# Last stage of a four-stage kernel: a new common order of steps, conditional waits between scatter-adds, tile loads ahead of the last store

## What is computed

```python
xf = x.reshape(-1, D)                                  # 4096 tokens, D = 256, after a layernorm
scores = jax.nn.softmax((xf @ gate_w.T).astype(jnp.float32), axis=-1)
top_vals, top_idx = jax.lax.top_k(scores, K)           # K = 2 of E = 8
w_dense = jnp.zeros((T, E), x.dtype).at[jnp.arange(T)[:, None], top_idx].set(weights)
h = jnp.einsum('td,ehd->teh', xf, W1)
y, g = jnp.split(h, 2, axis=-1)
eo = jnp.einsum('teh,edh->ted', y * jax.nn.silu(g), W2)
z = jnp.einsum('te,ted->td', w_dense, eo)
z = z + _gated_mlp(xf, Ws1, Ws2)
x = x + jnp.tanh(g_ffn[1]) * z
```

## Time and profile before

| quantity | value |
|---|---|
| median of 3 runs | 1089.26 us (1087.65 to 1091.56) |
| profiled execution | 1092.42 us |
| its span, from first to last instruction | 1090.7 us |
| busy in the span: PE, DVE, ACT, POOL | 958.1, 765.4, 574.4, 400.7 us |
| mean granted clock of PE | 0.937 of full speed |

### The profile page before, as it was taken

One profiled execution on the slowest core, in us unless ns is written; L12 is line 12 of the kernel. 1 busy time (PEld: TensorE's weight loads), 2 busy tenths in 40 slices (PEclk: granted clock), 3 DMA queues, 4 the chain that ended last, 5 costly groups with the idle time before them and its releaser, 6 DMA issues. The chain is left out here.

```text
span 1090.7 us, 22828 instructions
## 1 busy us (share of the span) xinstructions
PE 958.1 (88%) x6365; PEld 810.7 (74%) x6365; DVE 765.4 (70%) x2323; ACT 574.4 (53%) x1344; POOL 400.7 (37%) x571
## 2 busy tenths in 40 slices
PE   4999999999996679999999999954999885999990
PEld 3667666676664348999999999854877765999990
DVE  3677777777752436888888888867766566888880
ACT  1588888878884423443443444314553422666660
POOL 1011111111110013453453544435646352666775
PEclk9999999999998759999999999995999887999996
DMA  7666647466600401011010010200223343776773
GB/s 204 158 146 149 153 115 175 111 164 137 168 2 19 136 11 41 27 42 33 25 50 25 25 50 25 75 1 25 79 89 120 128 160 89 124 122 119 123 120 44
DMA packets 91811, 98.41 MB, mean 90 GB/s; under 512 B 14992, under 2 KB 85472, under 8 KB 91744
## 3 DMA queue, kind: packets, MB, share of 16 engines
q1 hardware_dynamic: 77504, 79.11, 27.9%
q0 software_dynamic: 13680, 17.84, 9.4%
q10 hardware_dynamic: 560, 0.66, 0.2%
HBM read 30.18 MB, written 59.01 MB: 82 GB/s over the span
## 5 line engine op out<-in xcount | busy, mean ns | idle before, releaser
L1646 POOL DMA_INDIRECT out<-early_weights,aim x71 | 110.8, 1560 | 69.1 <-ACT early_weights L1744 24.7
L1621 POOL DMA_INDIRECT sorted_rows<-m_z,slot_i x64 | 73.2, 1143 | 68.5 <-DVE m_z L1828 51.4
L1154 ACT ACTIVATE f_hidden<-c_hidden,f_b 128x256 f32<-128x256 f32 x128 | 53.7, 470 | 68.3 <-PE c_hidden L1343 68.3
L1341 PE MATMUL c_mlp<-f_w_hi,f_hidden_hi 128*128 128x256 f32 x256 | 80.6, 315 | 3.6 <-DVE f_hidden_lo L1272 3.6
L1341 PE MATMUL c_hidden<-y2T_hi,f_w_hi 128*128 128x256 f32 x256 | 77.1, 301 | 0.0
L1343 PE MATMUL c_mlp<-f_w_hi,f_hidden_lo 128*128 128x256 f32 x256 | 72.4, 283 | 0.0
L1342 PE MATMUL c_mlp<-f_w_lo,f_hidden_hi 128*128 128x256 f32 x256 | 72.4, 283 | 0.0
L1343 PE MATMUL c_hidden<-y2T_hi,f_w_lo 128*128 128x256 f32 x256 | 72.3, 282 | 0.0
L1342 PE MATMUL c_hidden<-y2T_lo,f_w_hi 128*128 128x256 f32 x256 | 72.2, 282 | 0.0
L760 PE MATMUL ps_probT<-ident,prob 128*77 128x128 f32 x512 | 68.7, 278 | 3.7 <-ACT prob L491 3.2
L760 PEld LDWEIGHTS ps_probT<-ident,prob 128*77 128x77 f32 x512 | 59.7, 151 | 14.4 <-ACT prob L491 10.5
(11 more groups left out here) (336 smaller groups left out, 3091.3 us busy)
## 6 DMA issues: line engine op xcount, KB each, us to landing
sorted_rows<-no_row SPq DMA_DIRECT2D x15, 2340.0 KB, 12.2
m_z<-sorted_rows SPq DMA_DIRECT2D x71, 130.0 KB
early_weights<-expert_chunks SPq DMA_DIRECT2D x8, 640.0 KB, 4.5
combT<-combineT_all SPq DMA_DIRECT2D x16, 256.0 KB, 2.3
slT<-slots_all SPq DMA_DIRECT2D x16, 256.0 KB, 2.5
out<-x_all SPq DMA_DIRECT2D x8, 512.0 KB, 6.0
x_all<-x SPq DMA_DIRECT2D x15, 256.0 KB, 11.3
f_w_stage<-L_xattn_w SPq DMA_DIRECT2D x4, 512.0 KB, 3.7
```

Source lines behind the costliest of these rows:

```text
L1154: last = act.activation(hf[:, q % 2, j, :], psH[:, q % 2, j, :], ACT.Relu, bias=fb1[:, c_:c_ + 1])
L1341: pe.matmul(out, lh, rh, start=start, stop=False, skip_group_check=shared)
L1621: pool.indirect_dma_start(out=sorted_rows[:, :], in_=zn[:, b % 3, t, :], in_offset=None, out_offset=bass.IndirectOffsetOnAxis(ap=slot_i[:, ...
L1646: pool.indirect_dma_start(out=self.out[:, :], in_=xo[:, i % XO, :], in_offset=None, compute_op=ALU.add, out_offset=bass.IndirectOffsetOnAx ...
```

## The change

Three things change, all in `phase_d`.

1. The list `order` is replaced. The same steps get other stages and another sequence. `expert_hi` moves from stage ROUTE to LATE, `places` and `weights` from SHARED to ROUTE, `scatter` from ROUTE to AHEAD, `tanh` from ROUTE to SHARED, `table` from LATE to SHARED, `up(.,1)` and `hidden(.,0)` from SHARED to ROUTE, `down(.,0)` and the chunks 1 and 2 of `hidden_lo` from LATE to SHARED.
2. The bit that makes POOL wait for tiles i-1 and i-2 is raised at a change of expert only if the two experts can meet. `expert_base` now keeps the counts after each block. The table compares the block in which the last 256 rows of one expert begin (`last_from`) with the block in which the first 256 rows of the next one end (`first_to`); if the former is the later one, no token can be in both. After the last expert the bit is never raised. This adds nine DVE operations to the table, three of them over 128x568 elements, before the bits are done.
3. SP issues the first four tile loads as soon as the table is done, and stores the last block of x after them.

```diff
-        base = sb("expert_base", [P, NE1])
+        base = sb("expert_base", [P, NBLK + 1, NE1])
...
-        order = [(SHARED, "silu", 1), (LATE, "down", 0), (LATE, "hidden_lo", 1), (SHARED, "hidden_hi", 0),
-                 (SHARED, "up", 1), (ROUTE, "z_hi"), (AHEAD, "later_stats"), (SHARED, "places"),
...
+        order = [(ROUTE, "z_hi"), (SHARED, "tanh"), (LATE, "expert_lo"), (SHARED, "hidden_lo", 0), (ROUTE, "z_lo"),
+                 (LATE, "down", 1), (LATE, "expert_hi"), (SHARED, "hidden_hi", 0), (AHEAD, "scatter"),
...
-            for b in range(NE1 - 4, NBLK):
+            for b in range(NE1 - 4, NBLK - 1):
                 base_out(b)
...
                 sp.dma_start(zn[:, 0, i % BT, :], sorted_rows[bass.ds(r, P), :]).then_inc(xz_in[i % BT].sem, 16)
+                if i == BT - 1:
+                    base_out(NBLK - 1)
...
-                dve.tensor_tensor(base[:], ranks[:, BT, :], base[:], ALU.add).then_inc(place_done.sem, 1)
+                dve.tensor_tensor(base[:, f + 1, :], ranks[:, BT, :], base[:, f, :], ALU.add).then_inc(place_done.sem, 1)
...
+                dve.scalar_tensor_tensor(out=late_end[:], in0=tiles[:], scalar=float(P), in1=late_end[:], op0=ALU.mult, op1=ALU.add)\
+                   .then_inc(t_step.sem, 1)
+                dve.tensor_tensor(past_block[:], ends, spread(late_end[:].rearrange("p (e a) -> p e a", a=1), 2, NBLK), ALU.is_le)\
+                   .then_inc(t_step.sem, 1)
+                dve.tensor_reduce(last_from[:], past_block[:], AX.X, ALU.add).then_inc(t_step.sem, 1)
+                dve.tensor_tensor(past_block[:], ends, spread(early_end[:].rearrange("p (e a) -> p e a", a=1), 2, NBLK), ALU.is_le)\
+                   .then_inc(t_step.sem, 1)
+                dve.tensor_reduce(first_to[:], past_block[:], AX.X, ALU.add).then_inc(t_step.sem, 1)
+                dve.tensor_tensor(meet[:, 0:NE1 - 1], last_from[:, 0:NE1 - 1], first_to[:, 1:NE1], ALU.is_le).then_inc(t_step.sem, 1)
+                dve.tensor_tensor(met, spread(tile_f[:].rearrange("p (i a) -> p i a", a=1), 2, NE1), per_tile(upto[:]), ALU.is_ge)\
+                   .then_inc(t_step.sem, 1)
...
+                dve.tensor_tensor(met, met, per_tile(meet[:]), ALU.mult).then_inc(t_step.sem, 1)
+                dve.tensor_reduce(meetings[:], met, AX.X, ALU.add).then_inc(t_step.sem, 1)
-                dve.tensor_tensor(flags[:, 1:XT], owner[:, 1:XT], owner[:, 0:XT - 1], ALU.not_equal).then_inc(t_step.sem, 1)
+                dve.tensor_tensor(flags[:, 1:XT], meetings[:, 1:XT], meetings[:, 0:XT - 1], ALU.not_equal).then_inc(t_step.sem, 1)
```

More of the change, by code:

```diff
@@ L1529, in phase_d @@
         AHEAD, ROUTE, SHARED, LATE = range(4)
-        order = [(SHARED, "silu", 1), (LATE, "down", 0), (LATE, "hidden_lo", 1), (SHARED, "hidden_hi", 0),
-                 (SHARED, "up", 1), (ROUTE, "z_hi"), (AHEAD, "later_stats"), (SHARED, "places"),
-                 (LATE, "hidden_lo", 2), (ROUTE, "scatter"), (SHARED, "hidden", 0), (AHEAD, "later_rstd"),
-                 (SHARED, "weights"), (LATE, "table"), (AHEAD, "rows_in"), (LATE, "down", 1), (SHARED, "hidden", 1),
-                 (LATE, "down", 2), (ROUTE, "logits"), (ROUTE, "z_lo"), (SHARED, "up", 2), (SHARED, "silu", 2),
-                 (SHARED, "hidden_lo", 0), (AHEAD, "zf_out", 0), (SHARED, "hidden_hi", 1), (AHEAD, "turn_z", 0),
-                 (ROUTE, "expert_hi"), (LATE, "result"), (ROUTE, "silu", 0), (ROUTE, "tanh"), (ROUTE, "top_two"),
-                 (ROUTE, "up", 0), (SHARED, "hidden_hi", 2), (SHARED, "hidden", 2), (AHEAD, "zf_out", 1),
-                 (LATE, "expert_lo"), (AHEAD, "turn_z", 1), (ROUTE, "ranks")]
+        order = [(ROUTE, "z_hi"), (SHARED, "tanh"), (LATE, "expert_lo"), (SHARED, "hidden_lo", 0), (ROUTE, "z_lo"),
+                 (LATE, "down", 1), (LATE, "expert_hi"), (SHARED, "hidden_hi", 0), (AHEAD, "scatter"),
+                 (SHARED, "silu", 1), (LATE, "down", 2), (AHEAD, "rows_in"), (SHARED, "silu", 2), (ROUTE, "logits"),
+                 (SHARED, "hidden", 1), (ROUTE, "later_rstd"), (AHEAD, "zf_out", 0), (SHARED, "hidden_hi", 1),
+                 (SHARED, "up", 2), (LATE, "result"), (ROUTE, "top_two"), (SHARED, "hidden_hi", 2),
+                 (SHARED, "table"), (AHEAD, "turn_z", 0), (ROUTE, "up", 0), (SHARED, "hidden", 2),
+                 (AHEAD, "turn_z", 1), (SHARED, "hidden_lo", 1), (ROUTE, "ranks"), (SHARED, "down", 0),
+                 (ROUTE, "later_stats"), (SHARED, "hidden_lo", 2), (ROUTE, "places"), (ROUTE, "silu", 0),
+                 (AHEAD, "zf_out", 1), (ROUTE, "up", 1), (ROUTE, "hidden", 0), (ROUTE, "weights")]
         def added(eng, i):
```

32 lines of the change are left out of this document (24 added, 8 removed).

## The result

| quantity | before | changed |
|---|---|---|
| median, same chip | 1088.80 us (4 runs, 1087.65 to 1091.56) | 1059.91 us (4 runs, 1056.26 to 1061.85) |
| ratio, 95% interval | | 0.9727 (0.9691 to 0.9763) |
| profiled execution, span | 1092.42, 1090.7 us | 1056.26, 1054.5 us |
| mean granted clock of PE | 0.937 | 0.953 |

The change makes the kernel 28.9 us faster. The forecast was 1055.6, the range 1050 to 1067, and faster was the most likely outcome. The time is 4.3 us above the forecast.

What follows compares the result with a forecast made beforehand. Expert half bound by PE's work, block half by waits for expert weights and `hidden_lo`, then a hole and late POOL. Gains 14.5 + 5.9 + 0.7 - 0.6 + 13.2 = 33.7 us: 1089.26 to 1055.6, range 1050 to 1067.

Steps and rivals of the forecast that it cites:

- turns: Block half, logits(1) to logits(7): with the new order turns run at PE's pace of 15.46 us, gaining 14.5 us.
- hole: Logits(7) to first `x_up`: falls from 43.1 to 37.2 us, a gain of 5.9, bounds 2.7 and 8.7.
- first `x_up` to last output: Expert half: 0.7 us gained by PE's clock being back at full, 0.6 lost by the later store.
- lag of the last add: POOL at the end: seven of eight waits at a change of expert go, gaining 13.2 us.
- A: Block half: some step placed with slack is late, turns take 16.9 us, 8.6 less gain, 1064; chance 0.13.
- E: Block half: `weights` waits for `tanh`, PE pauses each turn and its clock halves, slower than before, 1107; chance 0.03.
- The 0.6 that the forecast took off for the store: Start of expert half: last store, ahead of the fifth tile load, holds it up; 0.6 us lost, between 0 and 1.3.
- Rival C: Expert half: bits stay raised or POOL keeps its old pace for another reason; 13.2 us less gain, 1069; chance 0.06.
- B: End of block half: all nine table additions take 0.78 us each, 3.2 us more, 1059; chance 0.08.
- D: End of block half: last scatter, from 11.3 beside the table, is slow, so the first tile comes late; 1058; chance 0.05.
- part 1 of the forecast: Block half: one new turn followed step by step, with POOL's scatter of block b beginning 12.2 us after logits(b).

Runs made afterwards that it cites:

- e1: Kernel before with the new order list alone, old bits and old place of the last store: 1078.0 us, ratio 0.9805.
- e3: Kernel before with only `expert_hi` moved from stage ROUTE to LATE, in its old place in the list: 1083.34 us, ratio 0.9811.
- e7: Changed kernel with PE's read of the first tile's expert put ahead of its last waits: 1070.86 us, ratio 0.9732 against the kernel before.
- e5: Changed kernel with the last store of x ahead of the first tile loads, as before: 1073.65 us, ratio 0.9743 against the kernel before.
- e6: Changed kernel with 40 matmuls, sums thrown away, in PE's pause ahead of down(7,1): 1067.8 us, ratio 0.9708 against the kernel before.
- e4: Changed kernel with the bit raised at every change of expert, added table operations kept: 1084.64 us, ratio 0.9843 against the kernel before.
- e0: The changed kernel again, unaltered, on chip 6: 1066.8 us against 1101.17 for the kernel before there, ratio 0.9695.
- e8: The kernel before, unaltered, traced again on chip 8: 1104.78 us in its one run.

## Why the prediction was right, point by point

The two first traces differ by 36.2 us in their spans. By the marks:

| step | predicted | measured |
|---|---|---|
| turns, logits(1) to logits(7) | 14.5 | 107.32 - 93.27 = 14.05 |
| hole, logits(7) to first `x_up` | 5.9 | 43.13 - 38.03 = 5.10 |
| first `x_up` to last output | 0.7 - 0.6 = 0.1 | 150.85 - 151.43 = -0.58 |
| lag of the last add | 13.2 | 15.30 - 2.65 = 12.65 |
| sum in the last stage | 33.7 | 31.2 |
| ahead of the last stage, same code | 0 | 735.01 - 730.03 = 4.98 |

**The turns.** Right, place and size. PE never waits, a turn is 15.53 to 15.56 and not 15.46; six times 0.08 is the half us. It isn't the order's: e1, which has the order alone, has 15.45 to 15.48. Where it comes from is open. e3 shows that moving `expert_hi` alone brings PE's pace in three turns of six. Rivals A and E (turns of 16.9, or a pause in each) didn't happen. Yet on three chips one turn does stutter, for a reason that no rival had. That the forecast met a chip on which the changed kernel doesn't is luck: on chip 6 it takes 1066.8, just inside the range, with 9.7 us lost again in the turns, and the gain holds only because the kernel before is 12.4 us slower there too.

**The hole.** The mechanism was right to the order of its parts. The table took 11.25 us (11.4 by the sum of its additions), the pause 9.69 (9.9), and `result(7)` ended 35.1 after logits(7) (35.6). The mis-sized step is the last: I put the first transpose 0.1 after `result(7)` and the first `x_up` 1.5 later. It was 1.1 and 1.8. The 1.0 is the read of the first tile's expert, which in the old kernel hid behind the wait for the first tile; e7 takes it away. I had not asked what stands between PE's last wait and its first transpose. The tile itself was there in time, and e5 shows that it would not have been with the store ahead. The forecast took the 5.9 as one sum. The runs part it: the order alone gives as short a hole (37.41 in e1), and the longer table (3.5) and the earlier loads (3.3) about cancel.

**The start of the expert half.** Sign wrong, by 0.7 us. I took it that PE, busy again for 8 us, would have its full clock back. But it was not busy: between the two `down` and the first `x_up` it idled for most of 4 us, and the granted clock, back at full by 887, was at 0.50 from 892 to 896. By the windows the half clock lasts until about 896.7 here, 5.1 us into the expert half, and until about 918.7 before, 2.9 us into it. These are estimates from the means of 0.91 and 0.66. The 2.2 us more at half clock cost 1.1. e6 shows it cleanly, since there the clock was at full before that gap and fell behind it. The 0.6 that the forecast took off for the store didn't come (e5).

**The lag.** Right: seven of eight waits went, the one at tile 13 stayed, and the last add starts 2.65 after its output (3 expected). e4 shows that it is the bits. Rival C is out. The size of this term varies with the length of the eight waits: 11.6 to 16.1.

**Rivals B and D.** Neither came. The table is at the price of its parts, and the scatter beside it was done before the table, the loads being issued at 882.20. That scatter began 12.1 after logits(7), as part 1 of the forecast has it, and not at D's 11.3. The five of its issues that start beside the table took 0.96 or 0.97 us each. So the port that the Trainium skill speaks of ("SBUF — State Buffer", "SBUF: two separate sides") cost POOL nothing there that can be read off. The forecast made D the case to expect by that rule, which holds for certain DVE operations only; it hadn't asked whether the table's are among them.

**From the sum to the median.** The marks explain 31.2 us of the last stage. The medians differ by 28.9, the profiled executions by 36.2. The profiled one of before was 3.6 us above its median, that of the changed kernel 3.65 below, and 5.0 of these 7.3 lie ahead of the stage, where the code is the same. Of the 4.3 us by which I missed, 2.5 are the terms above; the rest is this spread. The 34.4 us of e0 would fit as well, if the kernel before stutters on chip 6 as it does in its one trace from chip 8: there it loses 13.5 (120.79 - 107.32), the changed one on chip 6 loses 9.7, so that 3.8 come on top of 31.2. No trace of the kernel before was taken on chip 6.

## What to carry to other kernels

When a step consumes a transfer, count in turns how long after its issue it stands in the engine's program; moving that one step (`expert_hi`) two turns later gave turns at PE's pace, three of six, without anything else. When a wait is taken away, list every instruction between it and the next useful one, register reads too, and look for the gaps behind it that are long enough to bring the clock down again. Compare stages by their own marks: the same code ahead of the stage varied by 7.8 us between executions, more than most of the terms here.

## What the runs showed of the hardware beyond that

- PE, ACT and DVE can all stand at once with no wait that the profile shows. In e8, PE was busy for 6.20 of 14 us, in steps of about 1.4 us, and DVE stood for 12.53 us at a stretch, while POOL issued 16 indirect DMAs without a pause. The cost was 9 to 13.5 us in eight traces on chips 5, 6 and 8. The one trace with such a row elsewhere, on the first chip, lost nothing. The cause is open.
- The same kernel takes 1088 us on two chips and 1100 on three. In its two traces from chips of either kind, a pause of 1.47 us between two scatters was there in the faster and not in the slower one. That this makes the difference isn't shown.
- Filling a pause with matmuls kept the granted clock at 1.00 (2.4 GHz) through it. But a gap of 2.56 us behind it was followed by 0.50, 0.3 us after PE had started again (e6).
